# First pass of a two-layer spectral and Sobel kernel: TensorE's program without its loop, and the mirror products halved on GpSimd

## What is computed

```python
# layer 0: a spectral convolution on 20 x 20 modes
def dht_2d(x):
    f = jnp.fft.fftn(x, axes=(2, 3))
    ff = jnp.fft.fftn(x[..., ::-1, ::-1], axes=(2, 3))
    result = f.real - ff.imag
    norm = jnp.sqrt(jnp.sum(result * result, axis=(2, 3), keepdims=True))
    return result / norm            # 0 where the norm is 0
x_ht = dht_2d(gn(x))
out_modes = compl_mul2d(x_ht[:, :, :20, :20], weights1)   # mixes 64 channels to 64
x = x + dht_2d(zero_padded(out_modes)) / (H * W)
# layer 1: depthwise Sobel magnitude
x = x + jnp.sqrt(gx * gx + gy * gy + 1e-8)    # gx, gy of gn(x)
```

## Time and profile before

| | before |
|---|---|
| median of 3 runs | 2676.01 us (2673.57 to 2676.49) |
| profiled execution: its own time | 2672.72 us |
| its span | 2670.9 us, 62478 instructions |
| TensorE busy | 2465.4 us (92%) |
| VectorE busy | 2052.7 us (77%) |
| ScalarE busy | 2053.7 us (77%) |
| GpSimd busy | 913.9 us (34%) |
| `pass1` | from the start to about 764 us |

### The profile page before, as it was taken

How to read it: one execution, slowest core, us unless ns; L and a number is a source line. 1 busy time by engine, 2 the same in 40 slices (tenths; PEclk the granted TensorE clock), 3 DMA queues, 4 the chain that set the end, 5 groups by cost and what they waited for, 6 DMA issues and landing times.

```text
span 2670.9 us, 62478 instructions
## 1 busy us (share of the span) xinstructions
PE 2465.4 (92%) x22236; PEld 1823.3 (68%) x22236; DVE 2052.7 (77%) x2783; ACT 2053.7 (77%) x3633; POOL 913.9 (34%) x533
## 2 busy tenths in 40 slices
PE   6988988898946679999999999999999999999998
PEld 5777777777736656666666666666666666666666
DVE  5988988898972468778778778778778777877776
ACT  6877877787842357887887888788788788788887
POOL 3433433444430223333333333333333333333332
PEclk9999999999968879999999999999999999999999
DMA  7766766666752315555555555555555555555554
GB/s 204 193 185 178 194 180 170 190 189 179 198 123 52 95 37 148 164 166 151 160 164 156 155 165 158 156 161 163 152 161 164 150 163 165 150 161 166 163 164 123
DMA packets 808909, 421.78 MB, mean 158 GB/s; under 512 B 20912, under 2 KB 807344, under 8 KB 807472
## 3 DMA queue, kind: packets, MB, share of 16 engines
q1 hardware_dynamic: 808624, 417.86, 55.3%
HBM read 283.56 MB, written 134.22 MB: 156 GB/s over the span
## 4 chain that ended last, share of the span: by engine, by line
PE 53%; ACT 5%; DVE 3%; issue 3%; ACTq 0%; DVEq 0%
PE g_ps L973 40%; PE y_ps L959 7%; PE v_ps L947 5%; ACT grad L1036 3%; ACT g_ps L1029 2%; DVE coef_t L1073 1%; DVE grad L1085 1%; PE v_ps L935 1%; ACT grad L1027 0%; ACT v_sb L1020 0%; ACT u_hi L1014 0%; DVE xbuf L1110 0%; DVE coef L1116 0%; DVEq L1110 0%; ACT coef_t L1043 0%
## 5 line engine op out<-in xcount | busy, mean ns | idle before, releaser
L973 PE MATMUL g_ps<-u_hi,stencil 128*128 128x512 f32 x2560 | 1053.7, 412 | 2.3 <-DVE grad L1085 2.2
L973 PE MATMUL g_ps<-u_lo,stencil 128*128 128x512 f32 x2560 | 1017.3, 397 | 0.0
L915 POOL TENSOR_TENSOR u_lo<-xbuf,u_hi 128x1024 fp32r<-128x1024 f32 x256 | 565.9, 2211 | 1138.4 <-ACT u_hi L1014 1138.4
L1110 DVE SCALAR_TENSOR_TENSOR xbuf<-xbuf,rows,grad 128x256 f32<-128x256 f32 x1024 | 575.5, 602 | 153.7 <-ACT grad L1036 153.5
L973 PEld LDWEIGHTS g_ps<-u_hi,stencil 128*128 128x128 f32 x2560 | 483.5, 189 | 306.8 <-issue 189.1
L973 PEld LDWEIGHTS g_ps<-u_lo,stencil 128*128 128x128 f32 x2560 | 481.6, 188 | 103.3
L1036 ACT ACTIVATE grad<-grad,eps,rows 128x256 f32<-128x256 f32 x1024 | 530.4, 595 | 0.1
L1027 ACT ACTIVATE grad<-g_ps 128x512 f32<-128x512 f32 x512 | 302.4, 591 | 291.7 <-PE g_ps L973 291.7
L1085 DVE TENSOR_TENSOR grad<-grad,g_ps 128x512 f32<-128x512 f32 x512 | 352.0, 687 | 223.8 <-ACT g_ps L1029 217.2
L277 POOL TENSOR_TENSOR m_lo<-xbuf,m_hi 128x512 fp32r<-128x512 f32 x256 | 306.2, 1196 | 436.7 <-ACT m_hi L381 436.7
L332 PE MATMUL t_ps<-first_sb,xbuf 128*64 128x64 f32 x8192 | 298.6, 229 | 86.6 <-issue 39.0
(11 more groups left out here) (116 smaller groups left out, 2171.8 us busy)
## 6 DMA issues: line engine op xcount, KB each, us to landing
xbuf<-x SPq DMA_DIRECT2D x256, 512.0 KB, 5.2
xbuf<-x SPq DMA_DIRECT2D x512, 256.0 KB, 3.1
out<-xbuf SPq DMA_DIRECT2D x512, 256.0 KB, 2.7
xbuf<-weights SPq DMA_DIRECT2D x8, 800.0 KB, 11.4
wmix<-weights SPq DMA_DIRECT2D x8, 800.0 KB, 14.0
second_sb<-second SPq DMA_DIRECT2D x1, 1230.0 KB, 8.4
mats_sb<-mats SPq DMA_DIRECT2D x1, 704.0 KB, 6.5
first_sb<-first SPq DMA_DIRECT2D x1, 32.0 KB, 5.5
```

Source lines behind the costliest of these rows:

```text
L915: nc.gpsimd.tensor_tensor(u_lo[:, r % 2, :, 1:W + 1], x_of(xbuf, r), u_hi[:, r % 2, :, 1:W + 1].bitcast(FP32), ALU.subtract)\
L973: mm = nc.tensor.matmul(g_ps[h][:, axis], stencil[:, m, :], u[:, r % 2, 4 * h:4 * h + 4, o:o + W], start=n == 0, stop=n == len(todo) - 1)
L1110: v = V.scalar_tensor_tensor(xs, xs, mean[:, bass.ds(group_planes(i, r, h, k), 1)], grad[:, r % 2, h, 256 * k:256 * (k + 1)], ALU.add, ALU ...
```

## The change

Three edits in `pass1`, and nothing elsewhere.

- TensorE's program calls `tile(i, i % 2)` for all 16 tiles in a Python loop, so that all its instructions are written out. The other engines keep their `Fori`.
- After m_lo of both halves of chunk k, GpSimd adds the columns 0 to 31 of chunk k-1's `prod` to its columns 32 to 63 and writes `folded` (128 x 16 x 32, two buffers). It waits for both products, and for the sum that read the buffer two chunks before. VectorE sums `folded` in place of `prod`, one chunk later (`sums(i, k - 1)` after the products of chunk k), and waits for the fold; before it overwrites a buffer of `prod` it waits until that has been folded.
- SyncE waits for `mirrored` (both products of the slot's chunk) in place of `chunk_done`.

```diff
--- before.py
+++ after.py
@@ -196,6 +196,7 @@
         x_lo = sb(ctx, "m_lo", [128, 2, HALF, RIGHT], FP32R)
         flips = sb(ctx, "flips", [128, 2, 128], FP32R)
         prod = sb(ctx, "prod", [128, 2, CHUNK, 64])
+        folded = sb(ctx, "folded", [128, 2, CHUNK, 32])
 
         edge = sb(ctx, "edge", [128, 2, TILE, 2, 2])
         edge_prod = sb(ctx, "edge_prod", [128, TILE, 2, 2])
@@ -223,6 +224,7 @@
         squared = sem("p1_squared")
         modes_out = sem("p1_modes_out")
         mirrored = sem("p1_mirrored")
+        fold_done = sem("p1_fold_done")
         edge_muled = sem("p1_edge_muled")
         edge_summed = sem("p1_edge_summed")
         tile_done = sem("p1_tile_done")
@@ -262,13 +264,21 @@
             with sp.Fori(0, NCHUNK // SLOTS - 1) as j:
                 for s in range(SLOTS):
 
-                    sp.wait_ge(chunk_done, j * SLOTS + s + 1)
+                    sp.wait_ge(mirrored, (j * SLOTS + s + 1) * 2 + 2)
                     load_chunk(sp, xbuf[:, s], x_p, j * SLOTS + s + SLOTS, x_in[s])
 
         @block.gpsimd
         def _(pool):
             for part in (x_hi, x_lo):
                 nc.gpsimd.memset(part[:, :, :, 0:RIGHT:RIGHT - 1].bitcast(FP32), 0.0).then_inc(padded, 1)
+
+            def fold(i, k):
+
+                pool.wait_ge(mirrored, i * HALVES + 2 * k + 4)
+                if not (is_first(i) and k < 2):
+                    pool.wait_ge(chunk_done, i * CHUNKS + k - 1)
+                p = prod[:, k % 2]
+                nc.gpsimd.tensor_tensor(folded[:, k % 2], p[:, :, 0:32], p[:, :, 32:64], ALU.add).then_inc(fold_done, 1)
 
             def tile(i, par):
                 for k in range(CHUNKS):
@@ -277,8 +287,13 @@
                         nc.gpsimd.tensor_tensor(x_lo[:, g, :, 1:65],
                                                 xbuf[:, k % SLOTS, HALF * g:HALF * (g + 1), 64:],
                                                 x_hi[:, g, :, 1:65].bitcast(FP32), ALU.subtract).then_inc(lo_ready, 1)
+                    if k:
+                        fold(i, k - 1)
+                    elif not is_first(i):
+                        fold(i - 1, CHUNKS - 1)
 
             over_tiles(pool, tile)
+            fold(TILES - 1, CHUNKS - 1)
 
         @block.tensor
         def _(pe):
@@ -356,7 +371,8 @@
                     if k == 1 and not is_first(i):
                         edges(i - 1, 1 - par)
 
-            over_tiles(pe, tile)
+            for i in range(TILES):
+                tile(i, i % 2)
             edges(TILES - 1, 1)
 
             pe.wait_ge(first_out, TILES * HALVES + 2)
@@ -446,6 +462,12 @@
                 row = rows[:, 0, bass.ds(i, 1), :]
                 nc.vector.tensor_tensor(row, row, edge_sum[:].unsqueeze(1), ALU.add).then_inc(tile_done, 1)
 
+            def sums(i, k):
+
+                dve.wait_ge(fold_done, i * CHUNKS + k + 1)
+                nc.vector.tensor_reduce(rows[:, 0, bass.ds(i, 1), CHUNK * k:CHUNK * (k + 1)],
+                                        folded[:, k % 2], axis=AX.X, op=ALU.add).then_inc(chunk_done, 1)
+
             def tile(i, par):
                 for k in range(CHUNKS):
                     slot = k % SLOTS
@@ -456,16 +478,20 @@
                         nc.vector.tensor_reduce(rows[:, 1, bass.ds(i, 1), p0:p0 + HALF], square[:, g],
                                                 axis=AX.X, op=ALU.add).then_inc(summed, 1)
                         dve.wait_ge(pe_mirror, i * HALVES + 2 * k + g + 3)
+                        if g == 0 and not (is_first(i) and k < 2):
+                            dve.wait_ge(fold_done, i * CHUNKS + k - 1)
                         nc.vector.tensor_tensor(prod[:, k % 2, HALF * g:HALF * (g + 1), 0:64],
                                                 xs[:, HALF * g:HALF * (g + 1), 0:64][:, :, ::-1],
                                                 z_ps[g][:], ALU.mult).then_inc(mirrored, 1)
-                    dve.wait_ge(mirrored, i * HALVES + 2 * k + 4)
-                    nc.vector.tensor_reduce(rows[:, 0, bass.ds(i, 1), CHUNK * k:CHUNK * (k + 1)],
-                                            prod[:, k % 2], axis=AX.X, op=ALU.add).then_inc(chunk_done, 1)
+                    if k:
+                        sums(i, k - 1)
+                    elif not is_first(i):
+                        sums(i - 1, CHUNKS - 1)
                     if k == 2 and not is_first(i):
                         edges(i - 1, 1 - par)
 
             over_tiles(dve, tile)
+            sums(TILES - 1, CHUNKS - 1)
             edges(TILES - 1, 1)
             dve.wait_ge(stats_pe, 1)
             for a, name in enumerate(("diffs", "s2")):
```

## The result

The changed kernel takes 2632.2 us (median of 4 runs, 2631.35 to 2633.34), beside 2674.8 us for the kernel before (median of 4 runs): a ratio of 0.9841 with a 95% interval of 0.9824 to 0.9858, or 42.6 us. The forecast was 52.3 us less than before and a range of 2613 to 2636. Its direction and range held; about 10 us are missing.

What follows compares the result with a forecast made beforehand. The prediction saw the first pass bound by a TensorE-ScalarE ring plus stalls at TensorE's six loop jumps; 49.3 us for the jumps and 3.0 for product waits, 52.3 off the 2676.0 median, gave 2623.7 us, range 2613 to 2636.

Steps and rivals of the forecast that it cites:

- TensorE's program without its loop: First pass: writing out TensorE's tiles removes six jumps of 8.2 us each (gaps, slow clock, restart), 49.3 us.
- The waits for a product: First pass: TensorE's 15 waits for VectorE's product, once a tile, go; worth 3.0 us, bounds 0 and 4.5.
- The fold at no cost: First pass: GpSimd's 128 additions, about 1.2 us each, fit in its 2.09 us of idle time; cost 0.
- The edge addition: VectorE's edge_sum addition, median 888 ns, would wait more for GpSimd, at worst 1.2 us a tile; cost 0.
- The slots at no cost: First pass: SyncE releasing a slot of x one to three us sooner is worth 0.
- nothing behind it moves but in step: End of the first pass: the later last sum costs 0, and all later work only shifts along with it.
- the rest of the kernel as it was: Sign to look for: the first pass 52 us shorter and everything outside it unchanged.
- GpSimd as the pace: Rival, first pass: folds from 3.3 us cancel the gain; at 3.6 us the time is 2714 us; 4 in 100.
- Other programs' jumps: Rival, first pass: hidden loop jumps of ScalarE, VectorE and GpSimd leave 21.6 us, giving 2645 us; 6 in 100.
- Gaps that stay: Rival, first pass: stops come with the amount of code, so only product waits go, giving 2673 us; 2 in 100.
- More than forecast: Rival, first pass: tiles close to TensorE's own 39 to 40 us, 35 us more gained, 2589 us; 3 in 100.
- the ring that paces a chunk: First pass: TensorE and ScalarE waiting on each other set 5.30 us a chunk; VectorE and GpSimd mostly stand outside.

Runs made afterwards that it cites:

- e1: The kernel before with only TensorE's first-pass program written out, no fold, slots released at the row sum: 2633.2 us, ratio 0.9835.
- e10: The kernel before with loads of x cut to one plane in eight after the first four chunks, later chunks computed from old data: 2664.5 us, ratio 0.9958.
- e11: The same cut of the loads of x as in e10, made on e2: 2662.0 us, ratio 0.995.
- e12: The changed kernel with 64 idle increments heading TensorE's program, and GpSimd doing each fold twice, once into a spare buffer: 2624.1 us, ratio 0.9805.
- e6: As e2, with the slots released at the sum again, which comes one chunk later: 2688.9 us, ratio 1.0055.
- e3: The changed kernel with 64 semaphore increments that nobody waits for at the head of TensorE's program, moving its later code: 2623.7 us, ratio 0.98.
- e7: The changed kernel with the 64 increments of e3, and ScalarE's copy of t_ps ahead of its square in each half: 2594.0 us, ratio 0.97.
- e2: The kernel before with the fold, the late sum and the early release of slots, TensorE's loop kept: 2684.8 us, ratio 1.003.
- e4: The kernel before with 158 increments ahead of TensorE's middle stage, moving the second pass's loop to its place in the changed kernel: 2686.0 us, ratio 1.0028.
- e9: The kernel before with 64 semaphore increments at the head of TensorE's program, the same edit as e3: 2662.9 us, ratio 0.9951.
- e5: The kernel before with only the early release of slots, at the products; TensorE's loop kept, no fold: 2670.0 us, ratio 0.9981.

## Why the prediction was right, and where it was not

- *TensorE's program without its loop.* Forecast 49.3 us; e1's first pass shows 48.4. That the four parts of it (two gaps, slow clock, restart) lie wholly on the path was right, and so was that no other engine's jump stands behind it: the changed kernel has tiles 42.1 to 42.2 us apart across the places of all six jumps.
- *The waits for a product.* Forecast 3.0 us; 2.4 between the traces of e1 and the changed kernel, 2.5 between the medians of e10 and e11. The 15 waits are gone. But 0.7 of the 2.4 come in tile 0, so the waits for a product are worth at most 1.7 of the 3.0.
- *The fold at no cost.* Right: one more fold per chunk costs 2.2 us in all (e12). In the changed kernel a fold starts at 175.28, directly behind the second m_lo, and ends 0.97 us before the next m_lo starts; all engines, timeline of the changed kernel:

```profile
174.13 1.20 POOL L287 TENSOR_TENSOR m_lo<-xbuf,m_hi 128x512 fp32r<-128x512 f32 x1 [0.82 <-ACT m_hi L397]
...
175.28 1.29 POOL L281 TENSOR_TENSOR folded<-prod 128x512 f32<-128x512 f32 x1
...
177.54 1.20 POOL L287 TENSOR_TENSOR m_lo<-xbuf,m_hi 128x512 fp32r<-128x512 f32 x1 [0.97 <-ACT m_hi L397]
...
179.08 1.15 PE L347 MATMUL t_ps<-first_sb,xbuf 128*64 128x64 f32 x32 [0.25 <-ACT tmodes L433]
```

- *The edge addition.* The direction was wrong. I had it wait more for GpSimd; it waits no longer at all (888 to 293 ns). The traces show why: before, an m_lo was under way at the start of 15 of the 16 additions, and each of the 15 ended 0.15 us after that m_lo did. In the changed kernel, where VectorE is earlier, none of the 16 meets a GpSimd operation. In e12 15 of them meet the second fold, take 0.90 to 1.11 us, and again end 0.15 us after it. It cost nothing either way.
- *The slots at no cost.* Right in the changed kernel; e6 shows that this holds only because the release moved with the sum.
- *The step that failed:* "nothing behind it moves but in step", and in the last part "the rest of the kernel as it was". Work behind the first pass does move in step, to 1 us, but TensorE's code does not stay where it was: the written-out pass shifts the body of the second pass's loop against the blocks in which code is fetched, and two jumps that had cost nothing came to cost 2.76 and 3.88 us and a spell of lower clock each, 10.4 us in all. I had looked for gaps at the other engines' jumps and not at TensorE's own in the stage that the change leaves alone. e3 takes this out and lands on the forecast (to the tenth by luck, as said at e3). That 2632.2 still lies in the range of 2613 to 2636 is luck too: its width was reckoned from the tile and the spread of the runs, and no rival or term allowed for code that moves in a later stage.
- *The rivals.* GpSimd as the pace: e12 shows 2.6 us of folds per chunk at a cost of 2.2 us in all, against the 3.3 worked out as the turning point. Other programs' jumps: none. Gaps that stay: none in the first pass. More than forecast: TensorE comes near its own pace (busy 39.63 of 40.46 us a tile) only with an edit of ScalarE's order (e7), as the sentence against that rival said.

## What to carry to other kernels

When one engine's program is written out, look at that engine's loops in the later stages too: their jumps may gain or lose gaps of 3 to 4 us by place alone, and a few idle instructions at a point where the engine waits anyway can put that right. Before lightening an engine, name the ring that paces a chunk: the fold was worth 2.4 us while ScalarE's square was in that ring, and 11 once it was out. The sum of the waits for issue alone can mislead, since first gaps are booked elsewhere when another semaphore came last: read the gaps from the timeline. Where a wait is moved later, move the release of its buffer with it.

## What the runs showed of the hardware

- A jump back over a long body costs TensorE a fetch of code, in pieces of 16 KB: the page of the kernel before lists 194 of them with 3.18 MB, and at each of the six jumps the trace's DMA packets have two that start 4.0 to 4.4 us apart (4.9 to 5.8 in e2). The Trainium skill, "Runtime: NRT & Kernel Launch", section "Instruction fetch mechanics", says that code comes in blocks of 256 instructions, in sequence, and that a taken branch to a block no longer held stalls. The trace agrees. e3, e4 and e9 show besides that how much of the target's block lies behind the target decides whether the next block shows as a gap. It is fetched in every case, 3.5 to 3.8 us after the first at the first jump of the second pass in the kernel before, the changed kernel, e3 and e4, and with 172 or more instructions left TensorE doesn't wait for it.
- With the count of e4 and an offset of some 60 instructions, all the places agree, to within a few instructions: 36 instructions are left in the piece at the first pass's jump before (two gaps) and 228 in e9 (one); at the second pass's jump 172 before and 206 in e3 (none), 14 in the changed kernel, e1 and e4 (2.65 to 3.88 us, once eight short matmuls have run). The offset was fitted, not measured.
- The first of the two fetches doesn't show at the second pass's jump. Ten long matmuls of 0.24 us stand there behind the last wait ahead of the branch, and four in the first pass; that this hides it fits the rows, but it wasn't tried by itself.
- A fetch at a jump takes longer while loads run: gaps of 4.03 and 2.69 us with the DMA engines at 0.80 of their time and 224 GB/s, 2.56 and 2.05 in e10. How the loads lie against the jumps moves the sum of the gaps, in e5 from 39.0 to 34.5 us and in e2 to 49.0; at five of the six jumps of e5 the first fetch's transfer starts before the gap does, in the kernel before 0.6 to 1.4 us into it. Why the early release alone brings it forward stays open.
- A VectorE addition with two SBUF inputs that meets a GpSimd operation takes longer: 293 ns alone, 0.83 to 1.31 us before and 0.90 to 1.11 in e12, and each ended 0.15 us after the GpSimd operation that was under way at its start.
